# Branch sums by POOL, paired units in product runs, pinned divisions, two score and four fill banks, maxima of two heads at once

## What is computed

```python
def _attn(q, k, v, mask=None):
    s = jnp.einsum('bhqd,bhkd->bhqk', q, k) / np.float32(np.sqrt(HD))   # HD = 64
    if mask is not None:
        s = jnp.where(mask, s, jnp.float32(-1000000000.0))
    return jnp.einsum('bhqk,bhkd->bhqd', jax.nn.softmax(s, -1), v)
...
o1 = _attn(q, k1, v1, causal[None, None])      # branch 0: all earlier keys
...
o2 = _attn(q, ks, vs)                          # branch 1: 256 selected keys
...
winmask = causal & (ii[:, None] - ii[None, :] < WINDOW)   # WINDOW = 64
o3 = _attn(q, kw, vw, winmask[None, None])     # branch 2: a window
o = g[:, 0] * o1 + g[:, 1] * o2 + g[:, 2] * o3
return o @ Wproj
```

## Time and profile before

| | us |
|---|---|
| median of three runs | 2780.64 (2779.1 to 2782.71) |
| the profiled execution | 2781.34 |
| its span from the first to the last instruction | 2779.4 |
| the attention stage, exact passes of 32 sides | 700.5 to 2379.8 |

### The profile page before, as it was taken

The page is one execution under the profiler, slowest core; times in us unless marked ns, Lnnn a source line. Parts: engine busy times, 40 slices in busy tenths (PEclk is TensorE's granted clock), DMA queues, the critical chain, the costliest instruction groups (busy, mean ns, idle before and its releaser), DMA issues. The chain is left out here.

```text
span 2779.4 us, 45396 instructions
## 1 busy us (share of the span) xinstructions
PE 2320.6 (83%) x16656; PEld 1545.5 (56%) x16656; DVE 1628.3 (59%) x3043; ACT 1266.2 (46%) x2777; POOL 669.8 (24%) x687
## 2 busy tenths in 40 slices
PE   5585858663999999999999999999999999601995
PEld 3464545442666666666666666566566666401884
DVE  4758575734466466466566576566565564450766
ACT  2354545440455555555455455555555555310442
POOL 0265656573011011011011011011010010145332
PEclk9697978765999999999999999999999999655997
DMA  2255555479547646556655565664664660611113
GB/s 97 97 219 184 216 187 201 172 269 226 126 93 146 132 101 139 122 118 131 127 121 122 120 136 114 136 129 104 137 137 96 138 130 10 158 39 47 48 53 110
DMA packets 222841, 360.53 MB, mean 130 GB/s; under 512 B 68794, under 2 KB 124701, under 8 KB 222240
## 3 DMA queue, kind: packets, MB, share of 16 engines
q1 hardware_dynamic: 216288, 348.43, 50.1%
q0 software_dynamic: 4320, 8.43, 0.9%
q10 hardware_dynamic: 2016, 0.77, 0.2%
HBM read 229.58 MB, written 126.56 MB: 128 GB/s over the span
## 5 line engine op out<-in xcount | busy, mean ns | idle before, releaser
L1370 ACT ACTIVATE prob<-ps 128x512 f32<-128x512 f32 (+5 forms) x1600 | 637.8, 441 | 665.8 <-PE ps L1325 656.3
L1434 DVE TENSOR_REDUCE maxima<-ps 128x1 f32<-128x512 f32 (+3 forms) x768 | 387.5, 547 | 291.4 <-PE ps L1250 147.0
L1344 PE MATMUL ps<-prob,plain 128*32 128x512 f32 (+5 forms) x3200 | 512.0, 443 | 0.0
L1400 POOL TENSOR_TENSOR products<-products,sums 128x256 f32<-128x256 f32 x192 | 140.8, 733 | 1540.3 <-DVE sums L1425 1539.0
L1439 DVE TENSOR_REDUCE maxima<-ps 128x2 f32<-128x512 f32 (+1 forms) x512 | 293.7, 606 | 192.6 <-PE ps L1261 98.4
L1425 DVE RECIPROCAL sums<-sums 128x256 f32<-128x256 f32 x192 | 331.9, 1736 | 97.6 <-ACT sums L1383 97.6
L1317 PE MATMUL ps<-q1a_s,k1a_s 128*128 128x512 f32 (+3 forms) x768 | 303.0, 395 | 0.0
L1325 PE MATMUL ps<-q1b_s,k1b_s 128*128 128x512 f32 (+3 forms) x768 | 301.1, 393 | 0.0
L1344 PE MATMUL ps<-prob,v_s 128*32 128x512 f32 (+3 forms) x1536 | 284.3, 491 | 0.0
L1250 PE MATMUL ps<-k1a_s,q1a_s 128*128 128x512 f32 (+3 forms) x768 | 234.5, 374 | 0.5 <-DVE maxima L1439 0.2
L1381 ACT ACTIVATE products<-ps,gates_a 64x512 f32<-64x512 f32 x192 | 131.0, 682 | 196.4 <-PE ps L1344 196.3
(11 more groups left out here) (333 smaller groups left out, 4889.8 us busy)
## 6 DMA issues: line engine op xcount, KB each, us to landing
qh_dram<-pairs SPq DMA_DIRECT2D x96, 512.0 KB, 2.7
kwh_dram<-pairs SPq DMA_DIRECT2D x64, 512.0 KB, 2.7
qa_s<-qh_dram SPq DMA_DIRECT2D x128, 256.0 KB, 4.7
kwa_s<-kwh_dram SPq DMA_DIRECT2D x128, 256.0 KB, 7.7
q1a_s<-qh_dram SPq DMA_DIRECT2D x128, 256.0 KB, 4.8
qb_s<-qh_dram SPq DMA_DIRECT2D x64, 256.0 KB, 9.3
kwb_s<-kwh_dram SPq DMA_DIRECT2D x64, 256.0 KB, 10.3
k1a_s<-k1ah_dram SPq DMA_DIRECT2D x32, 512.0 KB, 6.9
```

Of the source, the lines that this page charges most:

```text
L1344: mm = pe.matmul(ps[at:at + VD, SCORES + k % 2, q0 - c * CH:q0 - c * CH + w], w_, m.prob[:, n % PROBS, h, 0:w], start=first, stop=True, sk ...
L1370: act.activation(m.prob[:, u % PROBS, h, 0:w], ps[:, turn % SCORES, 0:w], ACT.Exp, scale=SCALE).then_inc(s["exp_done"], 1)
L1400: pool.tensor_tensor(o, o, m.sums[:, br, cc], ALU.mult).then_inc(s["divided"], 1)
L1434: ins = dve.tensor_reduce(partial[:, h, i, part:part + 1], bank[:, 0:w], AX, ALU.max)
```

## The change

Seven edits, all in `turns` and in the plan that it follows.

1. *Sums by POOL.* In branches 0 and 1 the ones no longer run on PE for each unit. POOL adds the exponentials of a sum's units into `acc` (12 additions and one copy a side, `SUMMING`). At the end of a branch a new step `total` multiplies `acc` by the ones (4 matmuls for each of the two branches, 8 a side, each 512 columns, in a fill bank), and a new step `take` lets ACT copy the result. Branch 2 keeps its ones.
2. *Pairs.* A unit of branch 1 or of the first half of branch 0 goes with one of the second half of branch 0 of the same width. Their four value matmuls fill the four column groups in one run. The windows come first in a side.
3. *Pinned divisions.* `pinned` gives divisions, projections, totals and the row step of branch 0 fixed slots, spread over both sides of a pair. `window` spreads the maxima by estimated DVE columns.
4. *Banks.* 2 for scores, 2 for products, 4 for fills. `prob` has 6 buffers.
5. *Maxima of two heads at once.* One step serves both heads. Head 0 uses rows 0 to 63 of the array, head 1 rows 64 to 127, into two fill banks. Only the queries' high part is taken. The masks still use all rows.
6. *Storage.* `qb`, `kwb`, `ksb`, `vw` and `vs` have one buffer instead of two; `q1a` and `qa` are stored with high and low halves swapped for head 1.
7. *Loads.* They are regrouped into `window_keys`, `window_exact`, `local`, `local_exact` and `whole`: 40 transfers a side, 32 before.

```diff
-SUMS = [(1, 0), (2, 0), (1, 1), (2, 1), (0, 0), (0, 1)]
-SCORES = 3
-SPARES = 3
+SUMS = [(2, 0), (2, 1), (1, 0), (1, 1), (0, 0), (0, 1)]
+def groups():
+    found = units()
+    sets = [found[2, c][i:i + 2] for c in range(NC) for i in range(0, len(found[2, c]), 2)]
+    short = found[1, 0] + found[1, 1] + found[0, 0]
+    return sets + [list(x) for x in zip(short, found[0, 1])]
+SCORES = 2
+SPARES = 4
 PIECES = 2
-PROBS = 4
+PROBS = 6
...
+    if w > 0:
+        pin((1,), [("rows", w, 0)])
+    if 0 < w:
+        if w % 2 == 0:
+            pin((0, 1), divisions(w - 1, 1, 1))
+        pin((2, 3), [("total", w - 1, 0), ("take", w - 1, 0)])
+        if w % 2 == 0:
+            pin((5, 6, 8, 9), divisions(w - 1, 0, 0) + divisions(w - 1, 0, 1))
+            pin((10, 13), [("proj", w - 1, c) for c in range(NC)])
+    if w < SIDES:
+        if w % 2 == 1:
+            pin((6, 8, 11, 13), divisions(w, 2, 0) + divisions(w, 2, 1))
+        pin((19, 20), [("total", w, 1), ("take", w, 1)])
+        if w % 2 == 1:
+            pin((22, 24), divisions(w, 1, 0))
...
                 if kind == "max0":
-                    h, i, part = a
+                    i, part = a
...
-                    mm = pe.matmul(bank[:, 0:k1 - k0], m.q1a[:, k, h, i * P:(i + 1) * P],
-                                   m.k1a[:, k, k0:k1], start=True, stop=True)
+                    last = [pe.matmul(both[h][:, 0:k1 - k0], m.q1a[r, k, h, i * P:(i + 1) * P], m.k1a[r, k, k0:k1],
+                                      start=True, stop=True, skip_group_check=True) for h, r in enumerate(upper)]
...
+                elif kind == "total":
+                    pe.wait_ge(s["acc_done"], len(SUMMING) * side + max(n for n, x in enumerate(SUMMING) if x[1] == a[0]) + 1)
+                    for c in range(NC):
+                        for h in range(HP):
+                            at = c * NW + h * VD
+                            mm = pe.matmul(both[0][at:at + VD, :], m.plain[:], m.acc[:, a[0], c, h, :], start=True, stop=True,
+                                           skip_group_check=True)
...
+                    if br == 2:
+                        product(side, u, 0, values)
+                        mm = product(side, u, NW, [m.plain[:]] * HP)
+                    else:
+                        mm = product(side, u, NW * place, values)
+                    mm.then_inc(s["products_done"], 1)
...
                     if u >= PROBS:
                         act.wait_ge(s["products_done"], u - PROBS + 1)
+                        old_side, old = divmod(u - PROBS, len(UNITS))
+                        if old in RELEASED:
+                            act.wait_ge(s["acc_done"], len(SUMMING) * old_side + RELEASED[old])
```

More of the change, by code:

```diff
@@ L2 @@
 from contextlib import ExitStack
+from itertools import accumulate
 import numpy as np
@@ new lines, with summing @@
+UNITS = sum(groups(), [])
+TOGETHER = [tuple(UNITS.index(x) for x in group) for group in groups()]
+LAST = [max(u for u, x in enumerate(UNITS) if x[:2] == k) for k in SUMS]
+LOCAL, WINDOWED = LAST[3] + 1, LAST[1] + 1
+OCCUPANTS = [-2, 0, 1, 2, 3, 1]
+def summing():
+    found, released, former = [], {}, {}
+    for u, (br, c, j, q0, w) in enumerate(UNITS):
+        if br == 2:
+            continue
+        if (br, c) not in former:
+            former[br, c] = u
+            continue
+        released[u] = len(found) + 1
+        if former[br, c] is not None:
+            released[former[br, c]] = len(found) + 1
+        found.append((u, br, c, former[br, c], q0 - c * CH, w))
+        former[br, c] = None
+    return found, released
@@ L1014, in preparation, with pinned, divisions, pin @@
     return todo + [("whole", side, 0)]
+def pinned(w):
+    def divisions(side, br, c):
+        return [("divide", side, SUMS.index((br, c)), piece) for piece in range(PIECES)]
+    slots = {}
+    def pin(at, steps):
+        for slot, step in zip(at, steps):
+            slots.setdefault(slot, []).append(step)
+    if w > 0:
[13 more added lines that the diff above has]
+            pin((22, 24), divisions(w, 1, 0))
+    return slots
@@ L1039, in exact_pass @@
-    return todo + pieces
-def window(w, prepare):
[L1045 to L1056, removed]
+            todo += [("acc", w, op) for op, x in enumerate(SUMMING) if x[0] == u]
@@ new lines, in exact_pass, with dve_columns @@
+        ready = [group for group, follower in zip(TOGETHER, TOGETHER[1:] + [(len(UNITS),)]) if follower[0] == u]
+        for group in ready:
+            todo.append(("products", w, group))
+            todo += [("sum", w, k) for k in sorted(LAST.index(x) for x in group if x in LAST)]
+        slots.append(todo + pins.get(u, []))
+    return slots
+def dve_columns(step):
+    if step[0] == "max0":
+        return HP * (min((step[3] + 1) * CH, (step[2] + 1) * P) - step[3] * CH + 120)
+    return {"max1": 2 * HP * KEEP + 120, "max2": 2 * HP * WN + 120, "rows": P, "whole": 0, "proj": CH, "divide": 1600}.get(step[0], -120) + 120
@@ L1140, in turn_no, with one, upper_and_lower @@
         return side // 2 + 1
+    def one(x, side, h):
+        return x[HP * NOPE * (side % 2) + NOPE * h:HP * NOPE * (side % 2) + NOPE * (h + 1)]
+    def upper_and_lower(first):
+        return [(h, at, comp + (lo ^ h)) for h in range(HP) for lo in range(2)
+                for at, comp in ((64 * lo, first), (64 * lo + 32, 4))]
     with nc.Block() as block:
@@ L1144, in _, with units_done @@
         def _(sp):
-            def local(side):
[L1146 to L1152, removed]
+            def units_done(side, count):
+                if side >= 0:
+                    sp.wait_ge(s["products_done"], len(UNITS) * side + count)
@@ L1217, in _ @@
                     carried(b + 1)
+            row(SIDES - 1, 0)
             store(B - 1)
@@ new lines, in product @@
+                n, k = side * len(UNITS) + u, SUMS.index((br, c))
+                first = UNITS.index(next(x for x in UNITS if x[:2] == (br, c))) == u
+                if first and side * len(SUMS) + OCCUPANTS[k] > 0:
+                    pe.wait_ge(s["banks_free"], side * len(SUMS) + OCCUPANTS[k])
+                for h in range(HP):
+                    mm = pe.matmul(ps[at + h * VD:at + (h + 1) * VD, bank_of(side, k), q0 - c * CH:q0 - c * CH + w],
+                                   weights[h], m.prob[:, n % PROBS, h, 0:w], start=first, stop=True,
+                                   skip_group_check=True)
@@ L1444, in _ @@
+                if plan.banks(step) > 1:
+                    continue
+                if kind == "rows":
                     br = step[2]
```

338 lines of the change are left out of this document (211 added, 127 removed).

## The result

The changed kernel takes 2797.44 us (median of 20 runs, 2781.15 to 2832.96), the kernel before 2782.36 (20 runs, 2778.63 to 2786.07). The ratio is 1.0053, with an interval from 1.0036 to 1.0069: slower by half a per cent, where 2707 had been forecast. The profiled execution is the shortest of its runs: 2781.15 us, span 2779.3. Its runs scatter over 51.8 us, seven times the 7.4 of before; that is a part of the answer.

What follows compares the result with a forecast made beforehand. PE alone was taken to set the pace (52.00 of 52.90 us a side); -3.9 + 6.5 - 5.8 + 1.1 - 0.4 = -2.5 us a side, -78 over 31 sides, -2 and +6 at the ends gave 2707 us, range 2610 to 2835.

Steps and rivals of the forecast that it cites:

- Products: PE's value products and totals: 5824 columns a side instead of 8128, saving 3.9 us a side.
- Maxima in halves: PE's maxima of two heads on row halves overlap, 6.7 us against 12.5, a gain of 5.8 us a side.
- A: Maxima on PE: halves overlap, division changes take most of it back; 2707 us, bounds 2611 and 2766, chance 0.55.
- C: Maxima on PE: the halves run one after the other; 2909 us, or 2813 with cheaper changes, chance 0.14.
- Changes of division: PE array's tiling: 34 more changes a side at 0.19 us each, +6.5 us a side.
- Waits: PE's waits: two score banks add 1.1 us a side, pinned divisions remove 0.4 at the projection.
- far under PE: DVE's busy time: 31.4 us in the odd side, 7 more than before in the even one, not limiting.
- under 0.5: PE's wait at the total for POOL's additions: under 0.5 us, since six `prob` buffers cover POOL's lag.
- E: Stage's sides: other work takes the place, a side stays at 52.8 us; 2785 us, chance 0.06.
- D: Two score banks expose ACT's copies and exponentials, PE waits 5 us a side at L1459; 2828 us, chance 0.18.
- The ends: Last side and what follows the stage: last side 2 us shorter, chain of total, copies and reciprocals 6 us longer.

Runs made afterwards that it cites:

- experiments 7: Changed kernel with ACT's copy of branch 1's total one slot earlier and maxima spread by score columns alone: 2725.73 us, ratio 0.9789.
- experiment 8: Changed kernel with maxima spread by score columns alone (divisions and projections weigh nothing), ACT's copy of the total left in place: 2715.81 us, ratio 0.976.
- experiment 9: Changed kernel with ACT's copy one slot earlier, maxima spread by score columns alone, and maxima on full rows, head after head: 2743.14 us, ratio 0.9861.
- experiment 10: Changed kernel with earlier copy, maxima spread by score columns, and `max2` masks head within tile (8 more division changes a side): 2752.29 us, ratio 0.9892.
- experiment 11: Changed kernel with earlier copy, maxima spread by score columns, and a tile's two narrow maxima parts handed out together: 2748.32 us, ratio 0.988.
- experiment 4: Kernel before with 2 score banks and 4 fill banks instead of 3 and 3: 2832.8 us, ratio 1.0192.
- The earlier take: Changed kernel with ACT's copy of branch 1's total one slot earlier, ahead of the exponential of unit 20: 2749.42 us, ratio 0.9877.
- experiment 2: Changed kernel with 8 `prob` buffers for the exponentials instead of 6: 2798.66 us, ratio 1.0035.
- experiment 6: Changed kernel with maxima over all 128 array rows, one head after the other: 2782.75 us, ratio 0.9996.

## Why the prediction was wrong

**Products: right.** 3.9 us a side were forecast, with 9.8 us left of 13.7. By the start-to-start times of PE's records, with a run's last group at 0.43 us for 512 columns, products and totals take 10.5 us a side in the changed kernel and in experiments 7 and 8, where 14.2 stood before: 3.7 less.

**Maxima in halves: the mechanism right, the size high.** The halves overlap (A, not C). Two partners' starts lie 0.003 us apart in the records, the eight 256-wide matmuls of `max1` take 0.67 us (1139.08 to 1139.75 in the timeline below) where eight one behind another would take 1.2 at the 0.15 of the earlier trace rows, and the pair of experiment 9 saves 0.23. The size of 5.8 us a side is shown only together with the changes: experiment 9 leaves 0.5 to 0.76 us with 27 changes against it, which at 0.10 to 0.16 each makes the halves alone worth 3.2 to 5.1, an estimate from experiments 9 to 11.

```profile
1139.08 0.74 PE L1392 MATMUL ps<-ksa_s,qa_s 64*128 64x256 f32 x8
1139.75 0.50 PE L1459 MATMUL ps<-q1a_s,k1a_s 128*128 128x512 f32 x1
```

**Changes of division: the mechanism right, the price high.** 0.19 was taken; 0.13 to 0.16 was measured for those of 192-wide maxima and masks in experiment 10, and 0.10 in experiment 11. The Trainium skill, "TensorEngine Tiling (Array Packing)", Key Properties, says that changing the mode drains TensorE; the runs agree that a change costs something, 0.10 to 0.16 us for drain and exposed weights together. The same page of the Trainium skill, Theoretical Speedup, names up to 2x for a contraction of 64 or less. The trace agrees for the pair of streams, whose starts lie 0.003 us apart; a side keeps 0.5 to 0.76 us of it. Halves and changes were both put too high, and in the sum the two errors offset each other in part, which is luck.

**Waits: the step that failed.** It said +1.1 a side for two score banks and -0.4 for the projection. Measured alone, two score banks cost 1.6 in the kernel before (experiment 4), 0.7 of it as waits for exponentials. With the fill evened (experiment 8) the forecast is nearly met: its waits are 28.2 us in 18 sides, 1.6 a side, which is the 0.9 of before plus 1.1 minus 0.4, its sides are 48.9 and 52.4 us, a mean of 50.6 against 50.3, and its time 2715.8 against 2707. PE's busy time fell there by 2.8 us a side, for 3.2 in the forecast (48.9 on average, where 51.7 stood). What the step left out, and so put at nothing, is the fill banks. I had costed DVE's busy time ("far under PE") and POOL's, and had looked for a wait at the total ("under 0.5"), where one of 0.2 indeed stands. I did not follow who holds a bank between PE's write and ACT's copy, nor how many pairs the plan hands out in between. It was in the plan: edit 3 of the change moves them. These waits are 28.6 us in 18 sides, 1.6 a side. The half clock behind them, up to 31 us in the stage, had no term either: the stage of before ran at 1.00, and I took that for given. Together they can be up to 51 + 31 us over 32 sides; the spans of the changed kernel and of experiment 8 are 63 apart (2779.3 and 2716.2), the medians 82.

**Which rival came.** E, "other work takes the place", forecast at 2785 with a chance of 0.06, is where the profiled execution lies (2781; the median is 12 above), by fill banks held too long. D is refuted as told: PE waits for exponentials by 1.2 us a side, not by 5.

**The ends: right in the sum.** Read in both traces from the first to the last exponential, the last side is 41.0 us long, where 41.7 stood: the 42.90 of the earlier trace rows reach 1.1 us past the last exponential (2378.66). So it is 0.7 shorter, and 2 was forecast. From the last exponential to the end of the span 405.9 us pass, where 400.7 did: +5.2 for a forecast of 6. Together that is +4.5 for +4. Against it the stage's first exponential starts at 690.9 us in this execution and at 699.7 in that of before; this start varies between 691 and 701 in the executions of the kernels above, so it is not put down to the change.

**What stays open.** Why the half clock comes behind this wait, and not behind the waits of up to 0.9 us of before, was not settled. The earlier take removed it in most sides and the evened fill in all, so that it comes with these waits is shown, and no more. The scatter of the changed kernel goes with the clock: its longest execution has a mean granted clock of 0.876 and its profiled one 0.893, which over their spans is 54 us of full clock lost for 52 us of time. The profiled execution of experiment 2 shows the form: the same waits, a span 30 us longer (2809.7), and 129.7 us at half clock between 750 and 2290 us, in stretches of up to 20.5 us. Open is why such stretches are short in one execution and long in the next, and why the median of the changed kernel lies 16 us over its profiled execution when that of full rows (experiment 6) does not.

## What to carry to other kernels

When a change turns single-bank steps into pairs, count banks at the place where a slow reader holds one: list, between the write and the release, every step that needs a bank, for each kind of side. A budget that spreads cover by another engine's load can pile it up where it does harm; where that engine was not the bound, as here, spreading by score columns alone was better by 82 us. And a tight PE can lose twice by a microsecond's wait, as it did here: the wait, and the clock behind it.

## What the chip showed that was not expected

- The granted clock fell to 0.50 for 3.42 us although PE had been busy for 14.64 of the 16.60 us before, with no wait longer than 1.2 us. The clock fell 15 times between 750 and 2290 us, 14 times for so long and once for 13.65 us, 61.4 us in all. In experiment 8 it did not fall once between 750 and 2290 us; PE was busy there for 1534 of the 1590 us from 700 us on.
- Executions of the changed kernel scatter by 52 us of 2797, and those of experiment 8, where the clock doesn't fall in this way, by 5 us of 2716. The falls alone do not make it: full rows (experiment 6) have 51.2 us of them and scatter by 9 us.
